# Two mixture layers: the turned and split x made once and read twice, and the top-8 taken in the logits' stage

## The chip, the cores and the metric

The program runs on one core of a Trainium2 chip. The metric is the device time of one launch in microseconds (us). The engines named below are PE (TensorE: matmuls and transposes), ACT (ScalarE), DVE (VectorE), POOL (GpSimd) and SP (SyncE, which only issues DMAs here).

## What is computed

Two transformer layers over 4096 tokens of width D = 256. Each is an attention followed by a mixture of experts, with a layer norm ahead of and behind each part. The change touches the mixtures alone. m0 is the mixture of the first layer and m1 that of the second:

```python
# m0 (xt: normalised tokens, H = 256, I = 512, E = 8, TOP_K = 2)
shared = jax.nn.silu(xt @ sg_w.T) * (xt @ su_w.T) @ sd_w.T
logits = xt @ router_w.T + routing_bias
topk_p, topk_idx = jax.lax.top_k(jax.nn.sigmoid(logits), TOP_K)
topk_p = topk_p / jnp.sum(topk_p, axis=-1, keepdims=True)
# routed = the experts' gated MLPs weighted by topk_p; output = shared + routed

# m1 (D = 256, routed H = 192, shared 2 * 192 = 384 wide, E = 8, K = 2, no bias)
scores = jax.nn.softmax((xf @ gate_w.T).astype(jnp.float32), axis=-1)
top_vals, top_idx = jax.lax.top_k(scores, K)
z = einsum(w_dense, experts) + _gated_mlp(xf, Ws1, Ws2)
```

## The kernel before

Tokens lie in T = 32 tiles of P = 128 rows. `core.x` and `core.y` are two arrays of 32 tiles that stay in on-chip memory (SBUF). x holds the running residual and y the output of a part until it is normed and added. Precision is kept by splitting: each float32 factor becomes a 16-bit high part and a 16-bit low part (what is left of it), and a product is three matmuls (high·high, low·high, high·low) or four.

One mixture runs five stages one after the other, each a block in which every engine has its own straight list of work, with semaphores between the lists. In the order of the profile's names, with m0's prefix:

- `m0ws` splits the shared expert's and the router's weights.
- `m0rl` (`router_logits`, from L2214) makes the router's logits. The 32 tiles go in 16 groups of two. Per group, DVE normalises two tiles (L2278), PE transposes them in four 128x128 blocks (L2235), ACT copies the transposes out of PSUM as the high part (L2269), DVE takes the low part (L2286), and PE multiplies both with the router in 32 matmuls of 8 columns each, 16 a tile (L2247). The high and low parts `m0rl_xt_high` and `m0rl_xt_low` have two buffers, which the next groups overwrite. DVE's list goes norm of group g+1, low of group g. PE's list goes turn of g+1, multiply of g. All 32 tiles' logits gather in one PSUM bank and DVE takes them out at the end in one instruction (L2303).
- `m0r` (`route`, from L2059) turns the logits into a place for every row in the experts' order. It is nearly all one chain on DVE. The bias row comes by a DMA that this stage issues and is added (L2139, m0 only). Then 32 MAX8 (L2142) give the eight largest logits of every token of a tile, and 32 max_index (L2145) their places. From L2147 on follow the counts and slots. Before its first instruction DVE waits for six constants that POOL makes (L2102 to L2110).
- `m0fs` (`shared_expert`, from L1597) runs the shared expert over 32 tiles in *slots* of one tile each. Beside it POOL sends each normalised row to its two places in `x_rows` in device memory (L1672), and SP, ACT and DVE load and split the routed experts' weights (`m0w_all`, L1707 and L1765), one piece per slot.
- `m0fx` (`routed_experts`) reads the sorted rows back and runs the routed experts.

In slot i of the shared expert, PE does the gate half of the up product of tile i, then its linear half (L1807, 24 matmuls of 128 columns each in m0, 18 in m1), then the transposes of tile i+2 (L1797, two per tile, called *turn*), then the down product of tile i-1 (L1807, 12 matmuls of 256 columns in m0, 9 in m1). ACT does silu of the gate (L1697), a weight piece's high part (L1707), a copy of tile i+2's normalised rows for the second send (L1692), the high part of its transposes (L1684) and the high part of the hidden values (L1703). DVE does the output of tile i-2 into y (L1760), the norm of tile i+3 (L1734), the weight piece's low part (L1765), silu times linear (L1748), the low part of the transposes of tile i+2 (L1741) and the low part of the hidden values (L1755). So every tile is normalised, transposed and split twice per mixture: once in `m0rl` and once in `m0fs`.

Turns of four slots are the unit of code: the first turn is written out, the other seven run in a hardware loop (`Fori`), and two closing slots follow. The logits' stage has such a loop too (six passes over two groups). Every engine's list is fixed by the code, so an engine that waits holds back all that stands behind it in its list.

## Time and profile before

| | us |
|---|---|
| median of 3 runs (2046.53 to 2051.81) | 2046.61 |
| the profiled execution, its own time | 2046.28 |
| its span in the trace | 2044.1 |

The sum of the prediction is made against the profiled execution, 2046.28 us. That is 0.33 us under the median, and 2.2 us of it lie around the span. The stages that the change touches, by the trace, from the first engine's entry to the next stage:

| stage | from to (us) | length |
|---|---|---|
| m0 logits | 256.0 to 284.8 | 28.8 |
| m0 route | 284.8 to 309.0 | 24.2 |
| m0 shared expert | 309.0 to 450.0 | 141.0 |
| m1 logits | 1635.5 to 1664.5 | 29.0 |
| m1 route | 1664.5 to 1686.5 | 22.0 |
| m1 shared expert | 1686.5 to 1814.0 | 127.5 |

Together they are 372.5 us of the span, and the rest of the program is the same code before and after. In the profile's rows an instruction stands with its start, its length, its engine and line, what it writes and reads, and, in brackets, how long the engine had been idle before it and what ended the wait. "issue" there means that nothing the profile shows was waited for, and "remote" that the last event came from elsewhere than a named instruction.

### The profile page before, as it was taken

The page shows a single profiled execution, that of the slowest core. Times are in us where ns is not written, and L with a number is a line of the kernel's source. Part 1 is how long each engine was busy: PE and PEld are TensorE (multiplying, and loading weights), DVE is VectorE, ACT ScalarE, POOL GpSimd, SP SyncE. Part 2 cuts the span into 40 slices and gives each one's busy share as a digit, 9 for nine tenths or more (in the row PEclk, how much of TensorE's full clock was granted, in tenths as well). Part 3 has the DMA queues.
Part 4 walks back from the last instruction along what each step waited for, and adds up shares of the span by engine and source line. Part 5 has one row for each costly group of instructions (what it writes and reads, how often), then busy time and mean ns, then how long its engine had stood idle before and what let it go on. Part 6 is the DMA issues. An engine that isn't in the chain of part 4 may idle for free. (4 is left out here: it accounts for less than half of the span.)

```text
span 2044.1 us, 43859 instructions
## 1 busy us (share of the span) xinstructions
PE 1667.6 (82%) x15250; PEld 953.9 (47%) x15250; DVE 1477.2 (72%) x2895; ACT 1098.1 (54%) x2248; POOL 418.3 (20%) x533
## 2 busy tenths in 40 slices
PE   2897259999999993767999999999997358889950
PEld 1775148976666662321222222222225247767740
DVE  4776677764444446869999999999936776656657
ACT  1443415643333332534999999999993415444422
POOL 2000206631222222220000000000000206534432
PEclk9998759999999996776999999999998759999985
DMA  5600004541111113332121111120005003323445
GB/s 200 276 0 6 31 1 153 157 125 48 60 58 61 58 53 127 119 94 54 37 60 48 47 47 45 48 60 24 17 17 175 24 1 110 113 87 120 126 148 174
DMA packets 113033, 164.09 MB, mean 80 GB/s; under 512 B 20246, under 2 KB 89756, under 8 KB 110556
## 3 DMA queue, kind: packets, MB, share of 16 engines
q1 hardware_dynamic: 97340, 117.85, 19.1%
q0 software_dynamic: 15520, 43.93, 5.9%
q8 instruction: 109, 1.79, 0.4%
q14 instruction: 64, 0.52, 0.1%
HBM read 89.07 MB, written 72.37 MB: 79 GB/s over the span
## 5 line engine op out<-in xcount | busy, mean ns | idle before, releaser
L1499 DVE TENSOR_REDUCE sa_row_max<-psum 128x1 f32<-128x1024 f32 x512 | 582.5, 1217 | 12.3 <-PE psum L1381 12.2
L1482 ACT ACTIVATE sa_probs<-psum 128x512 f32<-128x512 f32 x1024 | 549.6, 597 | 37.8 <-PE psum L1432 28.3
L1381 PE MATMUL psum<-v_k_max,v_q_stack 48*128 48x512 f16 x1024 | 301.4, 398 | 24.4 <-DVE sa_row_max L1499 16.2
L1412 PE MATMUL psum<-sa_probs,sa_v_now 128*32 128x256 f32 (+1 forms) x3840 | 321.0, 406 | 0.1
L1432 PE MATMUL psum<-v_q_stack,sa_k_main 49*128 49x512 f16 x1024 | 309.8, 384 | 2.0 <-ACT sa_probs L1482 1.2
L1993 PE MATMUL psum<-m0w_all,m0fx_xt_high 128*128 x568 | 193.4, 382 | 0.6 <-DVE m0fx_xt_low L1925 0.6
L1432 PEld LDWEIGHTS psum<-v_q_stack,sa_k_main 49*128 49x128 f16 x1024 | 64.6, 94 | 222.3 <-ACT sa_probs L1482 208.5
L1412 PEld LDWEIGHTS psum<-sa_probs,sa_v_now 128*32 128x32 f32 x3840 | 75.7, 108 | 189.9 <-issue 100.1
L1939 DVE TENSOR_TENSOR m0fx_ht_low<-psum,m0fx_ht_high 128x512 f16<-128x512 f32 x71 | 49.1, 692 | 134.4 <-ACT m0fx_ht_high L1907 134.4
L1901 ACT ACTIVATE m0fx_gate<-psum 128x512 f32<-128x512 f32 x71 | 42.4, 598 | 152.7 <-PE psum L1993 148.4
L1884 POOL DMA_INDIRECT y_rows<-m0fx_y_sb,m0fx_x_in x71 | 68.3, 962 | 274.1 <-DVE m0fx_y_sb L1946 274.1
L1306 POOL TENSOR_SCALAR sa_max_half<-sa_o_sb 128x128 f16<-128x128 f32 x32 | 9.3, 291 | 553.0 <-ACT sa_o_sb L1473 553.0
L1993 PE MATMUL psum<-m0w_all,m0fx_xt_low 128*128 x284 | 108.5, 382 | 0.0
L1993 PE MATMUL psum<-m0w_all,m0fx_ht_high 128*128 x568 | 104.6, 273 | 0.2 <-DVE m0fx_ht_low L1939 0.2
L1807 PE MATMUL psum<-m0fs_xt_high,m0s_all 128*128 128x128 f16 x1024 | 91.0, 220 | 1.3 <-issue 0.7
L1884 POOL DMA_INDIRECT y_rows<-m1fx_y_sb,m1fx_x_in x71 | 68.3, 962 | 102.3 <-DVE m1fx_y_sb L1946 101.1
L1807 PE MATMUL psum<-m0fs_xt_low,m0s_all 128*128 128x128 f16 x512 | 88.7, 220 | 0.4 <-issue 0.4
L1672 POOL DMA_INDIRECT x_rows<-m0fs_x_in,m_slots x64 | 75.8, 1184 | 47.6 <-ACT m0fs_x_in L1692 32.5
L1993 PE MATMUL psum<-m1w_all,m1fx_xt_high 128*128 x284 | 81.9, 330 | 0.6 <-DVE m1fx_xt_low L1925 0.6
L1807 PEld LDWEIGHTS psum<-m0fs_xt_high,m0s_all 128*128 128x128 f16 x1024 | 80.8, 99 | 2.1 <-DVE m0fs_xt_low L1741 0.9
L1993 PEld LDWEIGHTS psum<-m0w_all,m0fx_xt_high 128*128 128x128 f16 x568 | 56.0, 99 | 53.3 <-issue 2.7
L1381 PEld LDWEIGHTS psum<-v_k_max,v_q_stack 48*128 48x128 f16 x1024 | 55.0, 94 | 55.2 <-DVE sa_row_max L1499 46.7
(371 smaller groups left out, 3737.6 us busy)
## 6 DMA issues: line engine op xcount, KB each, us to landing
x_rows<-la_blank SPq DMA_DIRECT2D x18, 1032.0 KB, 8.2
v_q_stack<-q_scratch SPq DMA_DIRECT2D x192, 64.0 KB, 2.4
m0fx_x_in<-x_rows SPq DMA_DIRECT2D x71, 129.0 KB, 2.0
m1fx_x_in<-x_rows SPq DMA_DIRECT2D x71, 129.0 KB
m0fs_stage<-in_up SPq DMA_DIRECT2D x16, 512.0 KB
m0g_got<-y_rows SPq DMA_DIRECT2D x32, 256.0 KB, 3.8
o_scratch<-sa_o_sb POOLq DMA_DIRECT2D x32, 256.0 KB, 2.5
wo_o_in<-o_scratch SPq DMA_DIRECT2D x32, 256.0 KB, 3.6
```

Of the source, the lines that this page charges most:

```text
L1306: nc.gpsimd.tensor_scalar(max_half[n % 2][:, :], o_sb[n % 2][:, 0:P], 1.0 / MAX_SCALE, 1.0, ALU.mult, ALU.mult).then_inc(s["max_rounded"], 1)
L1381: nc.tensor.matmul(mx_ps[m % 2][:, half * 512:(half + 1) * 512], q_stack[h][side:side + ROWS, head, qt * P:(qt + 1) * P], k_max[side:side ...
L1412: last = nc.tensor.matmul(o_ps[32 * g:32 * g + 32, cols], v_now[:, kt, kv, :], probs[(GROUPS * step + g) % 16][:, cols], start=(kt == 0), ...
L1432: nc.tensor.matmul(st_ps[bank_of(at)][:, :], k_main[rows, kv, kt * P:(kt + 1) * P], q_stack[h][rows, kv * GROUPS + g, :], start=True, stop ...
L1482: nc.scalar.activation(probs[at % 16][:, :], st_ps[bank_of(at)][:, :], ACT.Exp, scale=0.25 / (QK_SCALE * QK_SCALE)).then_inc(s["expd"], 1)
L1499: nc.vector.tensor_reduce(row_max[n % 2][:, at % QT, column:column + 1], mx_ps[m % 2][:, :], AX.X, ALU.max).then_inc(s["maxed"], 1)
L1672: pool.indirect_dma_start(flat_rows, bass.IndirectOffsetOnAxis(ap=r.slots[:, i, c:c + 1], axis=0), x_in[i % UNROLL][:, c, :], None)\
L1807: last = nc.tensor.matmul(out, left(a, k), right(b, k), start=(m == 1), stop=(m == 3 * blocks))
L1884: pool.indirect_dma_start(y_rows, bass.IndirectOffsetOnAxis(ap=x_in[i % ROWS_HELD][:, D:D + 1].bitcast(I32), axis=0), y_sb[i % 2][:, :], N ...
L1901: nc.scalar.activation(gate[j][:, :], gate_ps[j][:, 0:F], ACT.Silu, scale=1.0 / W_SCALE)\
L1939: nc.vector.tensor_tensor(ht[j][1][0:ROWS, :, :], blocks(ht_ps[0:ROWS, 0:KF * P]), ht[j][0][0:ROWS, :, :], ALU.subtract).then_inc(s["ht_lo ...
L1993: last = nc.tensor.matmul(out, left(a, k), right(b, k), start=(m == 1), stop=(m == 3 * stop_at))
```

## The change

- `core.xt` is a second view of y: the 1024 bytes that a row of a tile has in y hold the high and the low part of its transposed tile, as 16-bit numbers.
- In the logits' stage, ACT's high part and DVE's low part go there, for all 32 tiles, and stay. PE reads them there in the logits' matmuls and again in the shared expert. When the shared expert's output of tile i-2 is done, it overwrites the tile's place in y.
- In the shared expert the transposes, their high part, their low part, two PSUM banks and three semaphores go. PE waits for neither the norm nor the split of a tile. Norm, copy and send of the rows to `x_rows` stay.
- The loops of the logits' stage and of the shared expert are written out on every engine. In the shared expert that is eight turns instead of one and a loop, and the two closing slots.
- The logits of each eight tiles (a *round* of four groups) go to one of two PSUM banks. DVE takes them out with the scale and the bias (`keep`, one instruction on 128x64), and does their 8 MAX8 (`maxima`) and 8 max_index (`find`). These three follow the low parts of groups 4q+5, 4q+6 and 4q+7 for rounds q = 0 to 2, and come at the end of the list for round 3.
- The bias row's DMA is issued at the start of the logits' stage. `route` loses it, the addition, and all MAX8 and max_index. It starts with what was L2147.

```diff
         self.y = ctx.enter_context(nc.sbuf_tensor("y", [P, T, D], F32))
+        self.xt = self.y[:, :, :].bitcast(F16).rearrange("p t (a k q) -> p t a k q", a=2, k=KD)
...
-    PEELED = 1
...
-        xt = [[ph.sb(f"xt_{x}{j}", [P, KD, P], F16) for x in ("high", "low")] for j in range(2)]
...
-        xt_ps = [ph.ps() for j in range(2)]
...
-            for k in range(PEELED):
-                turn(k)
-            with eng.Fori(PEELED, TURNS - PEELED) as k:
-                turn(k)
-            for k in range(TURNS - PEELED, TURNS):
+            for k in range(TURNS):
...
-                def high(i, j):
-                    act.wait_ge(s["x_turned"], i + 1)
-                    ge(act, s["lined"], i - 1)
-                    nc.scalar.activation(xt[j][0][:, :, :], xt_ps[j][:, 0:D].rearrange("p (k t) -> p k t", k=KD),
-                                         ACT.Copy).then_inc(s["xt_high"], 1)
...
                         again(i + 2, u + 2, k)
-                        high(i + 2, j)
...
-                    ge(dve, s["x_turned"], i - (UNROLL - 1))
                     ge(dve, s["x_again"], i - (UNROLL - 1))
...
-                def low(i, j):
-                    dve.wait_ge(s["xt_high"], i + 1)
-                    ge(dve, s["lined"], i - 1)
-                    nc.vector.tensor_tensor(xt[j][1][:, :, :], xt_ps[j][:, 0:D].rearrange("p (k t) -> p k t", k=KD),
-                                            xt[j][0][:, :, :], ALU.subtract).then_inc(s["xt_low"], 1)
...
-                    if real(i + 2):
-                        low(i + 2, j)
...
-                def turn(i, j, w):
-                    pe.wait_ge(s["x_ready"], i + 1)
-                    ge(pe, s["xt_low"], i - 1)
-                    for k in range(KD):
-                        last = nc.tensor.transpose(xt_ps[j][:, k * P:(k + 1) * P], x_in[w % UNROLL][:, 0, k * P:(k + 1) * P],
-                                                   core.ident[:, :])
-                    last.then_inc(s["x_turned"], 1)
...
-                def up(out, j, column):
+                def up(out, i, column):
...
-                                     lambda b, k: xt[j][b][:, k, :], KD)
+                                     lambda b, k: core.xt[:, i, b, k, :], KD)
...
                     if real(i):
-                        pe.wait_ge(s["xt_low"], i + 1)
                         ge(pe, s["silu_done"], i - 1)
-                        up(gate_ps[j], j, F).then_inc(s["gated"], 1)
+                        up(gate_ps[j], i, F).then_inc(s["gated"], 1)
                         ge(pe, s["hidden_done"], i - 1)
-                        up(lin_ps[j], j, 0).then_inc(s["lined"], 1)
-                    if real(i + 2):
-                        turn(i + 2, j, u + 2)
+                        up(lin_ps[j], i, 0).then_inc(s["lined"], 1)
                     if real(i - 1):
...
-            @block.sync
-            def _(sp):
-                if bias_row is not None:
-                    sp.dma_start(bias[:, :], bias_row.to_broadcast([P, E])).then_inc(bias_in, 16)
...
-                if bias_row is not None:
-                    dve.wait_ge(bias_in, 16)
-                    then(nc.vector.tensor_tensor(r.logits[:, :, :], r.logits[:, :, :],
-                                                 bias[:, :].unsqueeze(1).to_broadcast([P, T, E]), ALU.add))
-                for t in range(T):
-                    last = nc.vector.max(top[:, t, :], r.logits[:, t, :])
-                then(last)
-                for t in range(T):
-                    last = nc.vector.max_index(index[:, t, :], top[:, t, :], r.logits[:, t, :])
-                then(last)
...
+    ROUND = 4
+    xt = core.xt
...
+        def part(g, a):
+            return xt[:, g * G:(g + 1) * G, a, :, :].rearrange("p u k t -> p u (k t)")
...
+                def multiply(g):
                     pe.wait_ge(s["low"], g + 1)
+                    if g % ROUND == 0:
+                        ge(pe, s["kept"], g // ROUND - 1)
...
+                for g in range(NG):
+                    if g + 1 < NG:
+                        turn(g + 1)
+                    multiply(g)
...
+                    nc.scalar.activation(part(g, 0), turned(g % 2), ACT.Copy).then_inc(s["high"], 1)
...
+                    nc.vector.tensor_tensor(part(g, 1), turned(g % 2), part(g, 0), ALU.subtract).then_inc(s["low"], 1)
...
+                def keep(q):
+
+                    dve.wait_ge(s["logged"], (q + 1) * ROUND)
+                    at = slice(q * ROUND * G, (q + 1) * ROUND * G)
+                    given = logit_ps[q % 2][:, 0:ROUND * G * E].rearrange("p (t e) -> p t e", e=E)
+                    if bias_row is not None:
+                        ge(dve, s["bias_in"], 16)
+                        nc.vector.scalar_tensor_tensor(out=logits[:, at, :], in0=given, scalar=1.0 / W_SCALE,
+                                                       in1=bias[:, :].unsqueeze(1).to_broadcast([P, ROUND * G, E]),
+                                                       op0=ALU.mult, op1=ALU.add).then_inc(s["kept"], 1)
+                    else:
+                        nc.vector.tensor_scalar(logits[:, at, :], given, 1.0 / W_SCALE, None, ALU.mult)\
+                            .then_inc(s["kept"], 1)
+
+                def maxima(q):
+                    dve.wait_ge(s["kept"], q + 1)
+                    for t in tiles_of(q):
+                        last = nc.vector.max(top[:, t, :], logits[:, t, :])
+                    last.then_inc(s["maxed"], 1)
+
+                def find(q):
+                    dve.wait_ge(s["maxed"], q + 1)
+                    for t in tiles_of(q):
+                        last = nc.vector.max_index(index[:, t, :], top[:, t, :], logits[:, t, :])
+                    last.then_inc(s["found"], 1)
+                norm(0)
+                for g in range(NG):
+                    if g + 1 < NG:
+                        norm(g + 1)
+                    low(g)
+                    q, at = divmod(g - ROUND - 1, ROUND)
+                    if q >= 0:
+                        (keep, maxima, find)[at](q) if at < 3 else None
+                keep(NG // ROUND - 1)
+                maxima(NG // ROUND - 1)
+                find(NG // ROUND - 1)
+                dve.wait_ge(s["found"], NG // ROUND)
```

Three places of the order. On DVE in m0's logits stage, the loop's pass over two groups (its ISA rows are register instructions) before:

```order
L2278 TENSOR_SCALAR m0rl_xhat1<-x,mean_var,rstd 128x256
L2278 ISA x2
L2278 TENSOR_SCALAR m0rl_xhat1<-x,mean_var,rstd 128x256
L30 REGISTER_ALU
L2286 TENSOR_TENSOR m0rl_xt_low0<-psum,m0rl_xt_high0 128x512
L2278 ISA x2
L2278 TENSOR_SCALAR m0rl_xhat0<-x,mean_var,rstd 128x256
L2278 ISA x2
L2278 TENSOR_SCALAR m0rl_xhat0<-x,mean_var,rstd 128x256
L2286 TENSOR_TENSOR m0rl_xt_low1<-psum,m0rl_xt_high1 128x512
L2293 REGISTER_ALU
L2293 COMPARE_AND_BRANCH
```

and after, from the norm of group 6 to that of group 9, with the first round's three steps among them:

```order
L2227 TENSOR_SCALAR m0rl_xhat0<-x,mean_var,rstd 128x256 x2
L2233 TENSOR_TENSOR y<-psum,y 128x2x256
L2245 SCALAR_TENSOR_TENSOR m0rl_logits<-psum,m0rl_bias 128x64
L2227 TENSOR_SCALAR m0rl_xhat1<-x,mean_var,rstd 128x256 x2
L2233 TENSOR_TENSOR y<-psum,y 128x2x256
L2255 MAX m0l_top<-m0rl_logits 128x8 x8
L2227 TENSOR_SCALAR m0rl_xhat0<-x,mean_var,rstd 128x256 x2
L2233 TENSOR_TENSOR y<-psum,y 128x2x256
L2261 MAX_INDEX m0l_index<-m0l_top,m0rl_logits 128x8 x8
L2227 TENSOR_SCALAR m0rl_xhat1<-x,mean_var,rstd 128x256 x2
```

The low part now goes to y, and behind the low parts of groups 5, 6 and 7 stand the keep, the eight MAX8 and the eight max_index of tiles 0 to 7, ahead of the next norm.

On DVE in m0's shared expert, the first slot and the start of the second, before:

```order
L1734 TENSOR_SCALAR m0fs_x_in3<-x,mean_var,rstd 128x256
L1765 SCALAR_TENSOR_TENSOR m0w_all<-m0fs_stage,m0w_all 128x1024
L1748 SCALAR_TENSOR_TENSOR m0fs_hidden0<-psum,m0fs_gate0 128x512
L1741 TENSOR_TENSOR m0fs_xt_low0<-psum,m0fs_xt_high0 128x256
L1755 TENSOR_TENSOR m0fs_ht_low0<-m0fs_hidden0,m0fs_ht_high0 128x512
L1734 TENSOR_SCALAR m0fs_x_in0<-x,mean_var,rstd 128x256
L1765 SCALAR_TENSOR_TENSOR m0w_all<-m0fs_stage,m0w_all 128x1024
L1748 SCALAR_TENSOR_TENSOR m0fs_hidden1<-psum,m0fs_gate1 128x512
```

and after:

```order
L1718 TENSOR_SCALAR m0fs_x_in3<-x,mean_var,rstd 128x256
L1743 SCALAR_TENSOR_TENSOR m0w_all<-m0fs_stage,m0w_all 128x1024
L1726 SCALAR_TENSOR_TENSOR m0fs_hidden0<-psum,m0fs_gate0 128x512
L1733 TENSOR_TENSOR m0fs_ht_low0<-m0fs_hidden0,m0fs_ht_high0 128x512
L1718 TENSOR_SCALAR m0fs_x_in0<-x,mean_var,rstd 128x256
L1743 SCALAR_TENSOR_TENSOR m0w_all<-m0fs_stage,m0w_all 128x1024
L1726 SCALAR_TENSOR_TENSOR m0fs_hidden1<-psum,m0fs_gate1 128x512
```

The low part of the transposes is gone from between the product of silu and linear half and the hidden low part.

On PE in m0's shared expert, the end of the second slot, before (last up matmuls, turn of tile 3, down of tile 0):

```order
L1807 MATMUL psum<-m0fs_xt_high,m0s_all 128x128 x2
L1807 MATMUL psum<-m0fs_xt_low,m0s_all 128x128
L1797 MATMUL psum<-ident,m0fs_x_in 128x128 x2
L1807 MATMUL psum<-m0s_all,m0fs_ht_high 128x256
L1807 MATMUL psum<-m0s_all,m0fs_ht_low 128x256
L1807 MATMUL psum<-m0s_all,m0fs_ht_high 128x256 x2
```

and after, the third slot from its 48 up matmuls on, which now read y:

```order
L1772 MATMUL psum<-y,m0s_all 128x128 x48
L1772 MATMUL psum<-m0s_all,m0fs_ht_high 128x256
L1772 MATMUL psum<-m0s_all,m0fs_ht_low 128x256
L1772 MATMUL psum<-m0s_all,m0fs_ht_high 128x256 x2
L1772 MATMUL psum<-m0s_all,m0fs_ht_low 128x256
L1772 MATMUL psum<-m0s_all,m0fs_ht_high 128x256 x2
L1772 MATMUL psum<-m0s_all,m0fs_ht_low 128x256
```

The two transposes between the up and the down product are gone. The down product follows the linear half.

## Rows read from the trace of the kernel before

**Rows 1.** Windows: stretch and length, then busy time per engine (instructions), clock, DMA.

```profile
core 0: us, PE busy (x) PEld busy (x) DVE busy (x) ACT busy (x) POOL busy (x), PEclk, DMA share, GB/s
...
256.00:284.80 28.80, 24.83 (x320) 20.48 (x320) 21.47 (x49) 9.55 (x16) 0.00 (x0) 0.50 0.00 1
...
309.00:450.00 141.00, 137.65 (x1984) 131.12 (x1984) 104.76 (x190) 82.55 (x161) 84.07 (x95) 0.99 0.49 150
...
1686.50:1814.00 127.50, 113.09 (x1504) 101.38 (x1504) 81.48 (x190) 63.77 (x161) 72.04 (x95) 0.98 0.33 104
```

**Rows 2.** Groups by line, first logits stage: group, count, busy, mean ns, idle before.

```profile
L2286 DVE TENSOR_TENSOR m0rl_xt_low<-psum,m0rl_xt_high 128x512 f16<-128x512 f32 x16 | 11.1, 691 | 6.6 <-ACT m0rl_xt_high L2269 6.6
...
L2303 DVE TENSOR_SCALAR m_logits<-psum 128x256 f32<-128x256 f32 x1 | 0.4, 426 | 0.7 <-PE psum L2247 0.7
```

**Rows 3.** Timeline of DVE, first logits stage: start, us, instruction, [idle before <-releaser].

```profile
275.16 0.69 DVE L2286 TENSOR_TENSOR m0rl_xt_low<-psum,m0rl_xt_high 128x512 f16<-128x512 f32 x1 [0.68 <-ACT m0rl_xt_high L2269]
...
276.47 0.69 DVE L2286 TENSOR_TENSOR m0rl_xt_low<-psum,m0rl_xt_high 128x512 f16<-128x512 f32 x1
...
278.50 0.69 DVE L2286 TENSOR_TENSOR m0rl_xt_low<-psum,m0rl_xt_high 128x512 f16<-128x512 f32 x1 [0.67 <-ACT m0rl_xt_high L2269]
```

**Rows 4.** Timeline, start of both routing stages, to where their max_index runs end.

```profile
286.55 0.29 POOL L2110 TENSOR_SCALAR_AFFINE_SELECT m0r_before<-m0r_before 128x128 f32<-128x128 f32 x1
...
287.98 0.42 DVE L2139 TENSOR_TENSOR m_logits<-m_logits,m0r_bias 128x256 f32<-128x256 f32 x1 [3.14 <-DMA m0r_bias<-in_bias_r]
...
295.22 0.20 DVE L2147 CAST m0r_index_f<-m0r_index 128x64 f32<-128x64 uint32 x1
...
1666.16 0.58 DVE L2142 MAX8 m1r_top<-m_logits 128x8 f32<-128x8 f32 x7 [1.78 <-POOL m1r_before L2110]
...
1672.95 0.20 DVE L2147 CAST m1r_index_f<-m1r_index 128x64 f32<-128x64 uint32 x1
```

**Rows 5.** Timeline of PE, first work of the first shared expert.

```profile
308.84 1.12 PE L1797 MATMUL psum<-ident,m0fs_x_in 128*128 128x128 f32 x4 [9.98 <-DVE m0fs_x_in L1734]
...
310.46 0.39 PE L1807 MATMUL psum<-m0fs_xt_high,m0s_all 128*128 128x128 f16 x2 [0.51 <-DVE m0fs_xt_low L1741]
```

**Rows 6.** Timeline of PE, first shared expert: one turn and two slot ends.

```profile
353.40 0.39 PE L1797 MATMUL psum<-ident,m0fs_x_in 128*128 128x128 f32 x2
...
353.63 0.28 PE L1807 MATMUL psum<-m0s_all,m0fs_ht_high 128*128 128x256 f16 x1
...
354.84 0.27 PE L1807 MATMUL psum<-m0s_all,m0fs_ht_high 128*128 128x256 f16 x1
...
359.06 0.27 PE L1807 MATMUL psum<-m0s_all,m0fs_ht_high 128*128 128x256 f16 x1
```

**Rows 7.** Timeline of ACT, silu of two slots of the first shared expert.

```profile
352.71 0.58 ACT L1697 ACTIVATE m0fs_gate<-psum 128x512 f32<-128x512 f32 x1
...
356.80 0.58 ACT L1697 ACTIVATE m0fs_gate<-psum 128x512 f32<-128x512 f32 x1
```

**Rows 8.** Timeline of PE, second shared expert: last down matmuls of slots.

```profile
1705.41 0.27 PE L1807 MATMUL psum<-m1s_all,m1fs_ht_high 128*128 128x256 f16 x1
...
1708.63 0.27 PE L1807 MATMUL psum<-m1s_all,m1fs_ht_high 128*128 128x256 f16 x1
...
1808.66 0.27 PE L1807 MATMUL psum<-m1s_all,m1fs_ht_high 128*128 128x256 f16 x1
```

**Rows 9.** Waits in the second shared expert: us in total, times, longest.

```profile
ACT m1fs_xt_high L1684 <- remote: 17.3, 8, 3.3
...
PE psum L1807 <- issue: 9.0, 26, 0.5
...
PE psum L1807 <- DVE m1fs_ht_low L1755: 4.0, 9, 1.0
```

**Rows 10.** Waits in the first shared expert, same columns.

```profile
PEld psum L1807 <- issue: 1.7, 4, 0.5
```

**Rows 11.** Groups by line, second shared expert, the row scatter.

```profile
L1672 POOL DMA_INDIRECT x_rows<-m1fs_x_in,m_slots x64 | 65.5, 1024 | 47.1 <-ACT m1fs_x_in L1692 27.8 <-issue 8.0 <-DVE m1fs_x_in L1734 6.6
```

105 lines of the change are left out of this document (35 added, 70 removed).

## The prediction

> **What bounds the kernel now.** I read the table of windows first, stage by stage, since the share of busy time over the whole span mixes stages with different limits. In the first shared expert PE is busy 137.65 of 141.00 us at a clock of 0.99, and DVE, the next, 104.76 [rows 1]. So PE's list is the stage, and what leaves that list shortens it. In the second shared expert PE is busy 113.09 of 127.50 us: PE is still the longest list, but something stops it. In the logits stage PE (24.83) and DVE (21.47 of 28.80 us) are both high at half the clock, 0.50 [rows 1]. There I went to the groups by line and the timeline of DVE: before every second low part DVE waits 0.67 to 0.68 us for ACT's high part, nine times with 6.6 us in all [rows 2, 3]. So neither engine is full. A loop through PE, ACT and DVE sets the pace, 3.34 us for two groups (275.16 to 278.50). In the route stage all is one chain on DVE, so its rows can be subtracted one by one [rows 4].
>
> **Route: what goes.** In m0 the stage comes to the cast of the indices (L2147) at 295.22. What that cast needs besides the indices is POOL's last constant, done at 286.55 + 0.29 = 286.84 [rows 4]. The bias wait (3.14 us of idle), the addition, the 32 MAX8 and the 32 max_index lie between. So up to 295.22 - 286.84 = 8.4 us go. In m1 there is no bias and the constants have already been waited for: 1672.95 - 1666.16 = 6.8 us go [rows 4]. The bias DMA moves to the start of the logits stage, more than 10 us ahead of its first use, with nothing else in SP's list there: nothing. Together -15.2 us.
>
> **Logits: what comes.** MAX8 and max_index cost 6.79 / 32 = 0.212 us a tile [rows 4], 1.70 us for a round of eight. The keep of 128x64 has no row. It lies between nothing and the 0.43 of the keep of 128x256 [rows 2]; I take 0.20, the cast of the same shape [rows 4]. A round is 1.9 us. Rounds 0 to 2 (5.7 us) stand between the low parts, where DVE idles 2 x 0.68 us in four groups [rows 3], 4.1 us beside three rounds. If all idle time takes them, 5.7 - 4.1 = 1.6 us remain; if none, 5.7. A low part that is late delays PE's next turn and so the whole loop, and the two longer steps come singly in front of a norm, so one idle time does not cover a step wholly. I take 3.2, nearer to the low end, since the idle time is in the same list right behind. Round 3 stands at the end with nothing beside it: 1.9 less the old keep of 0.43, that is 1.5. Each logits stage gets 4.7 us longer (3.1 to 7.2), both 9.4 (6.3 to 14.4). Logits and route together: -15.2 + 9.4 = **-5.8 us** (-8.9 to -0.8).
>
> **First shared expert.** The turn's two transposes take PE from 353.40 to 353.63, that is 0.23 us [rows 6]. They stand in 30 of the 32 slots: 30 x 0.23 = 6.9 us, and the slot of 359.06 - 354.84 = 4.22 becomes 3.99. At the start the first transposes run at 308.84 and the first up matmul waits for the split until 310.46 [rows 5]. Up to 1.6 us of this go, less because the first matmuls then run longer at the low clock of the stages ahead; I take 1.2 (0.8 to 1.6). PE's queue stood still four times without a releaser, 1.7 us in all [rows 10]; as written-out code may keep or lose that, I take 0.9 (0 to 1.7). What is late next is the ring through ACT and DVE: silu, weight piece high, weight piece low, product, hidden high, silu. Between two silus it takes 356.80 - 352.71 = 4.09 us where the piece is 1024 wide [rows 7], 0.10 over the new 3.99. This ring loses from its ACT list the high part of the transposes and from its DVE list the low part, but both stand where these engines wait for each other, so I grant nothing. Half of the pieces are 1024 wide, so up to 16 x 0.10 = 1.6 us come back; since the two PSUM buffers let the narrow pieces make up for the wide ones, I take 0.5. Sum: -6.9 - 1.2 - 0.9 + 0.5 = **-8.5 us** (-10.2 to -6.1).
>
> **Second shared expert.** The same turns, -6.9, and the same start, -1.2. Then the waits. From 1705.41 to 1808.66 PE does 27 slots in 103.25 us [rows 8]. An undisturbed slot is 1708.63 - 1705.41 = 3.22, so 86.9 would do and 16.3 us are lost. 4.0 of them are PE waiting for the hidden low part, 9 times, and ACT waits in the same stage 17.3 us in 8 long waits that end with no named instruction, about one for each of the loop's seven passes and its entry [rows 9]. I read these as one thing: ACT comes late behind the loop's edge, then DVE, then PE. Written out there is no edge, so 4.0 go (bound: 0). The other 12.3 us are stand-stills of PE's own queue in the midst of a product ("issue", 9.0 us in 26 waits on the matmuls' row alone [rows 9]). No semaphore of the change touches these, so in the likeliest case I let them stay. Sum: -6.9 - 1.2 - 4.0 = **-12.1 us** (-8.1 if the waits stay).
>
> **The sum.** 2046.28 - 5.8 - 8.5 - 12.1 = **2019.9 us**, with its own bounds 2046.28 - 8.9 - 10.2 - 12.1 = 2015 and 2046.28 - 0.8 - 6.1 - 8.1 = 2031. The median of before is 0.33 us above the profiled execution, far inside these bounds.
>
> **Rival 1: the stand-stills of m1 go with the loop.** If PE's queue runs dry because of the loop's edges, 12.3 us more go: 2007.6. For it speaks that they hit the matmuls of m1's stage, most of which run in the loop. Against it: m0's stage has the same loop around the same kind of matmuls and shows four short ones [rows 9, 10]. The Trainium skill, Runtime: NRT & Kernel Launch, section Instruction fetch mechanics, states that an engine fetches its code ahead only in sequence, that a taken branch out of the fetched window makes it wait, and that kernels therefore prefer full unrolling; by that rule the time would be this rival's. The trace agrees with it in m1 only and not in m0.
>
> **Rival 2: writing out brings stand-stills, and the kernel is slower.** m1's slots lose 12.3 / 27 = 0.46 us each without a releaser. If what starves PE there is new code at a high rate of short instructions, then all 64 slots read new code after the change, while before only the first turns and the loop's first pass did. If m0's slots only reach m1's rate, 32 x 0.46 = 14.6 us come back: 2034.5, still faster. It decides from (26.4 + 6.1) / 64 = 0.51 us more in every slot of both mixtures on; with one us lost in every slot, m0 gains 32 and m1 17 us and the time is 2046.3 - 26.4 + 49 = 2069. Against it: m0's first turn is written out already, and its whole stage has four such waits [rows 10].
>
> **Rival 3: the row scatter becomes the bound in m1.** PE's slot there would be 3.22 - 0.23 = 2.99. POOL is busy 72.04 / 32 = 2.25 us a tile [rows 1], of which the two sends are 65.5 / 32 = 2.05 [rows 11], and every tile has three hand-overs between POOL, ACT and DVE. If these make a tile 3.22 long, DVE's norm (it waits until its buffer has been sent) holds up the hidden values behind it in DVE's list and the turns' 6.9 us are not gained: 2026.8. For it: a tile's steps come one after the other. Against it: 47.1 us of POOL's idle time, much of it waiting for ACT [rows 11], which loses work.
>
> **How the numbers follow.** Likeliest case 0.48 (2015 to 2031), rival 1 0.22 (2003 to 2010), rival 3 0.10 (2022 to 2031), m0 at m1's rate of stand-stills 0.08 (2030 to 2037). About 0.3% is what a measurement of this kernel can tell from no change. Within it (2040 to 2052) lies rival 2 with 0.35 to 0.6 us a slot, 0.07. Beyond it, slower, 0.05. So faster 0.88, same 0.07, slower 0.05. The range 2004 to 2034 leaves out the last two, a part of the m0 case and the low end of rival 1, together under 2 in 10.
>
> **What would show it.** Right: last down matmuls of neighbouring slots 3.99 apart in m0 and 2.99 in m1 where nothing stands; DVE's cast of the indices within 2 us of the route block's start; logits stages of 32 to 36 us; in m1 still some 20 "issue" waits of PE. Wrong: m0's slots at 4.1 or more (the ring binds), POOL with no idle time in m1 (rival 3), PE's "issue" waits gone (rival 1) or many of them in m0 (rival 2), or a logits stage over 36 us, where DVE would be the bound.

## The result

| | us |
|---|---|
| before, median of 5 runs (2046.53 to 2051.81) | 2049.20 |
| after, median of 4 runs (2028.17 to 2034.33) | 2031.59 |
| ratio after / before, 95% interval | 0.9913 (0.9893 to 0.9933) |
| forecast, ratio to the profiled run | 2019.9, 0.987 |

A fifth run of after took 4100.99 us at a granted clock of 1.0, which nothing here explains, and is left out.

The change is faster by 0.87% (0.67 to 1.07), 17.6 us by the medians. It was to be 26.4 us. The sign was right and the time lies within the range that was given, but a third of the expected gain is missing. The profiled execution of after took 2032.23 us (span 2030.2), so in the traces the gain is 13.9 us of span.

The profiled run of before, 2046.28 us, lies under all five timed ones. The first part of the program, which the change doesn't touch, took 243.1 us in it and 244.2 to 247.9 in the traces of all other kernels here.

This is the table of windows of after, the six touched stages in the order of [rows 1], with the columns of that group:

```profile
core 0: us, PE busy (x) PEld busy (x) DVE busy (x) ACT busy (x) POOL busy (x), PEclk, DMA share, GB/s
257.60:290.90 33.30, 24.61 (x320) 20.71 (x320) 28.16 (x148) 9.55 (x16) 0.00 (x0) 0.50 0.01 2
290.90:306.00 15.10, 2.12 (x6) 1.28 (x7) 11.17 (x40) 0.42 (x1) 1.22 (x7) 0.50 0.00 1
306.00:443.00 137.00, 132.12 (x1920) 124.96 (x1919) 93.94 (x160) 72.46 (x129) 79.65 (x96) 0.99 0.53 156
1629.30:1662.60 33.30, 24.62 (x320) 20.72 (x320) 28.16 (x148) 9.55 (x16) 0.00 (x0) 0.50 0.00 1
1662.60:1677.20 14.60, 2.05 (x5) 1.21 (x6) 10.68 (x38) 0.42 (x1) 1.15 (x7) 0.50 0.00 0
1677.20:1797.00 119.80, 107.47 (x1440) 96.89 (x1440) 69.25 (x160) 54.12 (x129) 73.96 (x96) 0.95 0.36 112
```

The same stages from the first instruction of each to the first of the next, before and after, from the timelines, with a second trace of after (experiment *again*):

| stage | before | after | again | change | forecast |
|---|---|---|---|---|---|
| m0 logits | 29.5 | 33.4 | 33.4 | +3.9 | +4.7 |
| m0 route | 22.9 | 14.6 | 14.6 | -8.4 | -8.4 |
| m0 shared expert | 142.9 | 137.8 | 141.6 | -5.1, -1.3 | -8.5 |
| m1 logits | 29.6 | 33.4 | 33.4 | +3.7 | +4.7 |
| m1 route | 21.0 | 14.2 | 14.2 | -6.8 | -6.8 |
| m1 shared expert | 129.1 | 120.4 | 124.0 | -8.8, -5.1 | -12.1 |
| sum | 375.1 | 353.7 | 361.1 | -21.3, -13.9 | -26.4 |
| all the rest of the span | 1669.0 | 1676.5 | 1671.1 | +7.4, +2.0 | 0 |

Route came as forecast and logits 0.8 to 1.0 us a stage better, and both repeat to 0.1 us. What is missing is missing in the shared experts, and these differ by 3.6 to 3.9 us each from one trace of the same kernel to the next. The rest of the span, whose code is the same, is longer by 2 to 7 us. Its parts moved the same way in unrelated kernels: m1's routed experts took 162.0 to 165.7 us over the fourteen traces, 162.8 before and 165.7 after.

In the logits stage of m0, on the timeline of DVE (start, length, instruction, idle time before it):

```profile
268.20 0.69 DVE L2233 TENSOR_TENSOR y<-psum,y 128x512 f16<-128x512 f32 x1
268.81 0.21 DVE L2245 SCALAR_TENSOR_TENSOR m0rl_logits<-psum,m0rl_bias 128x64 f32<-128x64 f32 x1
...
270.62 0.64 DVE L2255 MAX8 m0l_top<-m0rl_logits 128x8 f32<-128x8 f32 x8
...
276.06 0.69 DVE L2233 TENSOR_TENSOR y<-psum,y 128x512 f16<-128x512 f32 x1 [0.59 <-ACT y L2219]
...
286.92 0.69 DVE L2233 TENSOR_TENSOR y<-psum,y 128x512 f16<-128x512 f32 x1 [0.69 <-ACT y L2219]
```

The keep takes 0.21 us and eight MAX8 0.64. DVE waits before seven of the low parts instead of nine, 4.6 us in all where it was 6.6 [rows 2]:

```profile
L2233 DVE TENSOR_TENSOR y<-psum,y 128x512 f16<-128x512 f32 x16 | 11.0, 691 | 4.6 <-ACT y L2219 4.5
```

From the stage's start to its last low part it is 29.05 us against 27.15 before, so rounds 0 to 2 added 1.9 us where 3.2 were taken and 1.6 was the lower bound. From that low part to the route stage it is 4.38 against 2.36: the tail added 2.0 instead of 1.5, since round 2's max_index also stand behind the last low part (286.92). Ahead of the first keep two groups take 3.17 to 3.18 us (low parts at 260.49, 263.67 and 266.84) where they took 3.34 to 3.35 before (258.45, 261.80, 265.14): this stage's own pace is a little faster after the change, which the sum had at nothing; what makes it so was not taken apart. In the route stages, the first rows on DVE are these:

```profile
292.78 0.20 DVE L2088 CAST m0r_index_f<-m0l_index 128x64 f32<-128x64 uint32 x1 [2.05 <-POOL m0r_before L2061]
...
1664.17 0.20 DVE L2088 CAST m1r_index_f<-m1l_index 128x64 f32<-128x64 uint32 x1 [1.78 <-POOL m1r_before L2061]
```

They answer to [rows 4]: DVE now waits for POOL's last constant and nothing else.

PE's waits in the two shared experts, m0 first, then m1 (us in total, times, longest):

```profile
PE psum L1772 <- DVE m0fs_ht_low L1733: 3.3, 9, 1.3
...
PE psum L1772 <- issue: 1.1, 4, 0.4
```

```profile
PE psum L1772 <- issue: 5.9, 18, 0.5
...
PE psum L1772 <- DVE m1fs_ht_low L1733: 5.0, 8, 1.2
```

They answer to [rows 10] and [rows 9]. The waits for the hidden low part, of which m1's 4.0 us were to go, are 5.0 us now in m1, and 3.3 in m0 where they were 1.7.

### The profile page after: what moved, and what is told of

The parts are those of the page before. It is cut to its first block and busy times, and to the rows that moved or that the text cites. A ratio compares the mean times of both kernels' runs of the same rounds, so it can differ in the third digit from the quotient of the medians.

```text
span 2030.2 us, 42355 instructions
## 1 busy us (share of the span) xinstructions
PE 1658.7 (82%) x15122; PEld 946.4 (47%) x15122; DVE 1451.0 (71%) x2836; ACT 1079.1 (53%) x2184; POOL 415.6 (20%) x533
## 3 DMA queue, kind: packets, MB, share of 16 engines
q1 hardware_dynamic: 97340, 117.85, 19.4%
## 5 line engine op out<-in xcount | busy, mean ns | idle before, releaser
L1772 PE MATMUL psum<-y,m0s_all 128*128 128x128 f16 x1536 | 93.3, 221 | 10.4 <-PEq L2050 9.5
L1772 PEld LDWEIGHTS psum<-y,m0s_all 128*128 128x128 f16 x1536 | 90.3, 99 | 12.3 <-issue 11.6
L1772 PE MATMUL psum<-y,m1s_all 128*128 128x128 f16 x1152 | 76.8, 225 | 14.5 <-PEq L2050 9.4
```

Source lines behind the costliest of these rows:

```text
L1772: last = nc.tensor.matmul(out, left(a, k), right(b, k), start=(m == 1), stop=(m == 3 * blocks))
```

## Where a slot loses time

The measure for all that follows is taken from the timeline of PE: the time from the last down matmul of slot 0 to that of slot 31, less what undisturbed slots would take. These are 3.99 us in m0 and 2.99 in m1 without the turns (4.22 and 3.22 with them), the last one 2.76 and 2.13 (2.35 and 1.98 where the hidden values go first). What is lost ahead of the end of slot 0 is not in this measure. The kernels marked "m1 only" differ from after in m1 alone, so their m0 is after's once more.

| kernel | m0: slot 0 to 31, lost | m1: slot 0 to 31, lost |
|---|---|---|
| before | 130.6, 1.8 | 117.5, 19.2 |
| after | 127.2, 4.8 | 111.2, 19.4 |
| again (after) | 130.8, 8.3 | 115.0, 23.2 |
| loops | 124.5, 2.1 | 119.1, 27.2 |
| ahead | 124.1, 2.0 | 110.4, 18.7 |
| spaced | 124.1, 1.7 | 111.1, 19.3 |
| ahead_spaced, best | 123.6 and 123.7, 1.6 and 1.7 | 112.1 and 111.4, 20.4 and 19.8 |
| before_spaced | 129.1, 0.3 | 111.9, 13.6 |
| old_shared | 131.9, 3.1 | 116.5, 18.2 |
| no_scatter (m1 only) | 131.7, 9.3 | 91.9, 0.1 |
| sp_sends (m1 only) | 129.3, 6.9 | 91.9, 0.1 |
| pool_plain (m1 only) | 126.9, 4.5 | 91.9, 0.1 |
| half_sends (m1 only) | 125.8, 3.3 | 91.9, 0.1 |

A stretch of after's m1 in which PE stands still, first POOL, then PE on the same microseconds:

```profile
1699.08 0.20 POOL L1660 COPY m1fs_x_in<-m_tail 128x4 f32<-128x4 f32 x1
1699.55 0.98 POOL L1666 DMA_INDIRECT x_rows<-m1fs_x_in,m_slots  x1 [0.28 <-issue]
1700.84 0.96 POOL L1666 DMA_INDIRECT x_rows<-m1fs_x_in,m_slots  x1 [0.30 <-issue]
1701.80 0.20 POOL L1660 COPY m1fs_x_in<-m_tail 128x4 f32<-128x4 f32 x1
1702.28 0.98 POOL L1666 DMA_INDIRECT x_rows<-m1fs_x_in,m_slots  x1 [0.28 <-issue]
```

```profile
1699.06 0.50 PE L1772 MATMUL psum<-y,m1s_all 128*128 128x128 f16 x6
1699.80 0.27 PE L1772 MATMUL psum<-y,m1s_all 128*128 128x128 f16 x2 [0.24 <-issue]
1700.51 0.27 PE L1772 MATMUL psum<-y,m1s_all 128*128 128x128 f16 x2 [0.44 <-issue]
1701.26 0.38 PE L1772 MATMUL psum<-y,m1s_all 128*128 128x128 f16 x4 [0.48 <-issue]
1702.00 0.22 PE L1772 MATMUL psum<-y,m1s_all 128*128 128x128 f16 x1 [0.36 <-issue]
1702.72 0.60 PE L1772 MATMUL psum<-y,m1s_all 128*128 128x128 f16 x4 [0.50 <-issue]
```

PE does one to six matmuls of a product, stands for 0.24 to 0.50 us with no semaphore to wait for, and does the next. Beside it POOL sends rows without a pause. In the windows around it (columns as in [rows 1]) it shows what that costs twice:

```profile
1690.00:1696.40 6.40, 6.32 (x94) 5.81 (x92) 3.45 (x9) 3.25 (x8) 5.22 (x8) 1.00 0.40 132
1696.40:1702.60 6.20, 3.57 (x32) 2.08 (x29) 1.76 (x4) 1.21 (x3) 4.75 (x8) 1.00 0.44 133
1702.60:1709.50 6.90, 6.08 (x44) 4.84 (x45) 3.78 (x9) 2.04 (x5) 3.17 (x4) 0.51 0.23 73
1709.50:1720.00 10.50, 10.07 (x151) 9.49 (x149) 5.52 (x12) 4.94 (x12) 6.56 (x9) 1.00 0.37 115
```

From 1696.4 to 1702.6 PE does 32 matmuls where the stretch before had 94 in about the same time, and then TensorE's granted clock is 0.51, the lower of its two levels, until 1709.5. Slot 5 takes 9.07 us.

## The experiments

The theories at the start were those of the prediction: stand-stills that go with the loop (rival 1), that come with new code (rival 2), the row sends as the bound (rival 3), and, for m0's longer slots, the wide weight pieces. Each kernel was timed beside before, and its ratio is to before's runs of that time.

**again.** The same kernel.

> The changed kernel once more, nothing altered, to see whether PE's stand-stills have a place. In its first trace the down products of slots 0 and 31 of the second shared expert end 111.2 us apart where 30 undisturbed slots of 2.99 and the last of 2.13 would take 91.8: 19.4 us lost, 6.1 of them in slot 5 alone. In the first shared expert 127.2 against 122.5: 4.8 lost, 2.0 in slot 1. If the stand-stills belong to a place in the code: the same slots stand for about as long, slot 5 of m1 at 8 to 10 us, 17 to 21 us lost in m1. If they come from what else happens to go on at that moment: other slots stand, and the loss differs by several us. Time 2028 to 2034 us either way.

Measured: 2036.95 us (2031.55 to 2040.42) where before took 2050.36, ratio 0.9919 (0.9892 to 0.9947). Now slot 1 of m0 takes 9.55 and slot 1 of m1 8.44 us, and m1's slot 5 takes 4.47. So the stand-stills have no fixed place in the code. They come in the first slots, more often than not, and then in changing places of m1.

**loops.** One part of the change undone:

```diff
-            for k in range(TURNS):
+            turn(0)
+            with eng.Fori(1, TURNS - 1) as k:
                 turn(k)
+            turn(TURNS - 1)
```

> The changed kernel, but with the shared expert's hardware loop kept: first and last turn written out, six passes between, PE reading y by the loop's counter. If m1's stand-stills come from the loop's edges (rival 1 of the prediction), writing out should have removed them, which it did not; then this kernel loses about as much as the changed one or more, 19 to 25 us in m1, plus about 4 us of waits of PE for the hidden low part behind the edges: 3 to 8 us slower than the changed kernel. If they come from fresh code (rival 2), code that repeats has few: under 10 us lost in m1 and under 3 in m0, 8 to 12 us faster than the changed kernel. If they depend on neither: within 3 us of it.

Measured: 2035.67 us, ratio 0.9918 (0.9890 to 0.9947), beside again's 0.9919. PE's waits in m1:

```profile
PE psum L1774 <- issue: 12.7, 39, 0.4
...
PE psum L1774 <- DVE m1fs_ht_low L1735: 3.9, 8, 1.0
```

The loop has 27.2 us of loss in m1 (again 23.2, after 19.4). In m0 it has 2.1 (8.3 and 4.8), but slot 0 ends 12.2 us into the stage (after 9.2, again 9.6), since PE waits 2.92 us there for the hidden low part. Writing the shared expert out is worth nothing that these runs can tell, and code that repeats stands still as often as new code. Rivals 1 and 2 both fall.

**ahead.** ACT's and DVE's slots in another order:

```diff
 # ACT
                         silu(i, j)
-                        cut_high(k, u)
                     if real(i + 2):
                         again(i + 2, u + 2, k)
                     if real(i):
                         hidden_high(i, j)
+                        cut_high(k, u)
 # DVE
+                    if real(i):
+                        multiply(i, j)
                     if real(i - 2):
                         finish(i - 2, j)
                     if real(i + 3):
                         norm(i + 3, u + 3, k)
                     if real(i):
-                        cut_low(k, u)
-                    if real(i):
-                        multiply(i, j)
-                    if real(i):
                         hidden_low(i, j)
+                        cut_low(k, u)
```

> The changed kernel, but in each slot of the shared expert the hidden values go ahead of the weight piece: ACT does silu, row copy, hidden high, weight piece high; DVE does silu times linear, output of tile i-2, norm of tile i+3, hidden low, weight piece low. Same instructions, other order. In the changed kernel's trace every fourth slot of m0 takes 4.32 to 4.37 instead of 3.99 us, with PE waiting for the hidden low part (3.3 us in m0, 5.0 in m1). If that comes from the two wide weight pieces that stand in the way of the hidden values (the ring that the prediction priced at 0.5 us): m0's slots all become 3.99, 2.5 to 3.3 us less in m0, 3 to 5 less in m1, 5 to 8 us faster than the changed kernel. If PE's waits only follow from its own stand-stills, or the weight pieces now come late: no gain, or the next stage starts later, within 2 us of it. The stand-stills without a releaser (13 to 15 us in m1) stay in both.

Measured: 2023.67 us (2020.74 to 2026.65), 13 us less than again beside it, where 5 to 8 were expected. The ratio to before, 0.9847, has a wide interval (0.9774 to 0.9920). All slots of m0 but slot 4 (6.01 us) are 3.99. In m1 18.7 us are still lost.

**no_scatter.**

```diff
                     for c in range(2):
...
+                        if filled is None:
+                            nc.gpsimd.memset(unsent[:, 2 * i + c:2 * i + c + 1], 0.0).then_inc(sent[i % UNROLL], 16)
+                            continue
                         pool.indirect_dma_start(flat_rows,
```

> The changed kernel without the sends of rows to x_rows in m1 alone; the POOL instructions that sent are replaced by a memset of one column each. It leaves out that the second mixture's routed experts see the rows, so their part of the output is not computed. If the sends (64 indirect DMAs beside PE's stream, and the descriptors that POOL writes for them) make PE's queue stand still in m1: its loss falls from 19.4 to under 5 us and the time by 12 to 17 us. If rival 3 (the scatter as the bound) holds, PE's waits for the hidden low part go with it, 5 us. If neither: 15 us or more are still lost without a releaser, and the time changes by less than 4 us.

Measured: 2012.51 us. The window of m1's shared expert:

```profile
1680.80:1781.50 100.70, 97.86 (x1440) 93.92 (x1440) 69.74 (x160) 55.05 (x129) 10.85 (x96) 0.98 0.17 49
```

That is 100.7 us instead of 119.8, every slot 2.99, 0.1 us lost, and the waits for the hidden low part are down to two, 1.8 us in all. So all of m1's stand-stills come with the sends, and the waits are for the most part their shadow.

**spaced.** One wait more on POOL:

```diff
                     ge(pool, sent[i % UNROLL], i // UNROLL * 32)
+                    ge(pool, s["gated"], i - 1)
                     nc.gpsimd.tensor_copy(x_in[i % UNROLL][:, :, D:ROW], r.tail[:, i, :, :]).then_inc(s["tail_set"], 1)
```

> The changed kernel with one wait more on POOL: before tile i's row copy and two sends it waits until PE has done the gate product of tile i-2, so that the sends come two per slot with a pause behind them and never four or more in a row. Every row is still sent. Without any sends in m1 its loss there was 0.1 us instead of 19 to 23, so the sends make PE stand; the gaps in the traces lie on the third and later of sends that follow each other in 1.3 to 1.5 us. If the run of sends is what counts: m1 loses under 5 us, the clusters in the first slots of m0 (2 to 6 us) go too, and the time falls by 12 to 20 us against the changed kernel, to 2012 to 2020. If the mere number of sends counts: still over 12 us lost in m1, and no gain.

Measured: 2025.73 us, ratio 0.9887 (0.9857 to 0.9918). The windows of the two shared experts:

```profile
304.90:439.60 134.70, 130.83 (x1920) 125.20 (x1920) 93.17 (x160) 72.87 (x129) 77.45 (x96) 0.98 0.54 158
```

```profile
1672.20:1792.70 120.50, 106.54 (x1440) 96.55 (x1440) 69.73 (x160) 54.16 (x129) 70.96 (x96) 0.96 0.36 111
```

Half right. m0 is 134.7 us long, and apart from slot 1 (5.65) all its slots are 3.99. m1 still loses 19.3 us, where under 5 were expected. But there the wait did not make the pause that it was for. POOL and PE in m1, as POOL comes to send two pairs one behind the other:

```profile
1694.61 0.96 POOL L1667 DMA_INDIRECT x_rows<-m1fs_x_in,m_slots  x1 [0.30 <-issue]
...
1696.22 0.98 POOL L1667 DMA_INDIRECT x_rows<-m1fs_x_in,m_slots  x1 [0.46 <-issue]
1697.51 0.96 POOL L1667 DMA_INDIRECT x_rows<-m1fs_x_in,m_slots  x1 [0.30 <-issue]
```

```profile
1698.29 0.49 PE L1773 MATMUL psum<-y,m1s_all 128*128 128x128 f16 x6 [0.32 <-issue]
1699.03 0.89 PE L1773 MATMUL psum<-y,m1s_all 128*128 128x128 f16 x13 [0.24 <-issue]
```

Call it a run where sends start less than 1.8 us after one another. m1 of *spaced* has nine runs of four or more sends, and the like kernels *ahead_spaced* and *best* below have ten and nine. All of PE's "issue" waits there (24, 31 and 28) lie between the third send of a run and 1.5 us behind its last, a stretch of about a third of the stage, and every run has some. Pairs that stand alone have none. In m1 of after (18 waits), again (27) and before (26) too, all lie in runs of three or more. So where PE stands speaks for the run, and m1's loss does not speak against it. A pair needs 2.7 us (1.29 and 1.44 from send to send), so a slot of 2.99 leaves hardly any pause. No kernel here makes pauses in m1 with both indirect sends, so rate and run are not told apart by a test of their own.

*spaced* also takes away what *ahead* was to explain. After has 4.32 to 4.37 us in every fourth slot of m0 (again up to 4.41), and the wide weight pieces are the same in spaced. The rows of ACT, first of after, then of spaced, at such a slot:

```profile
343.95 0.60 ACT L1685 ACTIVATE m0fs_gate<-psum 128x512 f32<-128x512 f32 x1 [1.48 <-PE psum L1772]
344.45 1.05 ACT L1695 ACTIVATE m0w_all<-m0fs_stage 128x1024 f16<-128x1024 f32 x1
...
347.93 0.58 ACT L1685 ACTIVATE m0fs_gate<-psum 128x512 f32<-128x512 f32 x1
```

```profile
341.44 0.60 ACT L1686 ACTIVATE m0fs_gate<-psum 128x512 f32<-128x512 f32 x1 [0.88 <-PE psum L1773]
341.93 1.05 ACT L1696 ACTIVATE m0w_all<-m0fs_stage 128x1024 f16<-128x1024 f32 x1
...
345.43 0.60 ACT L1686 ACTIVATE m0fs_gate<-psum 128x512 f32<-128x512 f32 x1
```

From silu's start to the end of the hidden low part it is 4.84 us in after and 4.82 in spaced, and from silu to silu 3.98 and 3.99. The ring keeps up, but with nothing to spare at a slot of 3.99. What differs is silu's start: 0.86 us behind the gate product's last matmul in after, 0.26 in spaced, with nothing in the rows that ACT could have waited for. It is the same in all of these slots of after (six) and again (seven): silu comes 0.81 to 0.90 us behind that matmul, and the second of two sends 1.46 us apart starts 0.58 us ahead of it. In spaced the second send starts 1.6 us ahead of that matmul in the same slots, and silu comes 0.26 us behind it. So the delay goes with where the sends lie, and the ring without slack passes it on to PE. How a send reaches ACT was not taken apart.

**before_spaced.** The same wait in the kernel before.

> The kernel before the change with the same one wait on POOL. It shows what the change is worth where nothing stands still. If runs of sends made the stand-stills of before too: m1 loses under 5 of its 16 to 18 us over slots of 3.22, m0's 1.8 at slot 3 go, and the time is 2026 to 2034. The change between the two spaced kernels is then what the prediction's sum gives without stand-stills and with the late hidden parts: 9 us less for logits and route, 6 to 8 for m0's shared expert, 7 to 10 for m1's, some 22 to 26 in all. If the wait holds the turns up (PE reads the norm's buffer here, which is only free after a send): slower than 2040.

Measured: 2040.53 us, ratio 0.9960 (0.9946 to 0.9974). m0 loses 0.3 us, m1 13.6. Between the two spaced kernels the change is worth 14.8 us, not 22 to 26: m0's shared expert 6.8 and logits with route 7.5 by the traces, but m1's shared expert only 2.6. From slot 0 to 31 m1 takes 111.9 us with the turns and 111.1 without.

**ahead_spaced, best.** Both edits together, timed twice.

> The two edits together: hidden values ahead of the weight pieces, and sends at the pace of the slots. Hidden first alone gave about 10 us against the changed kernel. If the causes are separate (weight pieces in the way of the hidden values in m0; runs of sends that stop PE in m1 and in the first slots), every slot of both mixtures is undisturbed: m0's slots all 3.99 and m1's all 2.99, under 2 us lost in each, 2004 to 2012 us. If m1's waits for the hidden low part were only the shadow of the sends, the sum is less than both: 2012 to 2018.

> The kernel of ahead_spaced again (hidden values ahead of the weight pieces, sends at the pace of the slots), timed in more rounds beside the kernel before. The changed kernel stood at 0.9913 and 0.9919 of before. If the two edits add something that can be measured: 0.985 to 0.989 of before. m0's slots are 3.99 but for one of the first three; m1 again loses about 20 us, since two sends a slot are still more than PE bears.

Measured: 2023.40 us, ratio 0.9873 (0.9850 to 0.9895), and 2021.76 us, ratio 0.9879 (0.9859 to 0.9899). Both lie above what was expected of the two edits. They add nothing to each other that can be measured (ahead 2023.67, spaced 2025.73): each alone has made all of m0's slots but one whole, and neither helps m1. This is a version ahead of both kernels, 24 and 28 us under before by the medians.

**sp_sends, pool_plain, half_sends.** What about the sends stops PE. In m1, SP sends the same bytes to a fixed place; or POOL does so with plain DMAs; or POOL makes one of the two indirect sends. The first two leave out that the rows go to their experts' places, the third the second copy of each row. The edits, with SP's and the counters' waits left out here:

```diff
 # sp_sends, behind each weight piece on SP
...
+                                sp.dma_start(x_rows[2 * i + c, :, :], x_in[i % UNROLL][:, c, :])\
+                                    .then_inc(sent[i % UNROLL], 16)
 # pool_plain
+                            pool.dma_start(x_rows[2 * i + c, :, :], x_in[i % UNROLL][:, c, :])\
+                                .then_inc(sent[i % UNROLL], 16)
 # half_sends
                             pool.wait_ge(s["x_again"], i + 1)
+                            if filled is None:
+                                continue
...
```

> The changed kernel, in m1 with the same rows and bytes sent by SP's plain DMAs, tile after tile in a fixed place of x_rows, in place of POOL's indirect DMAs. It leaves out that the rows go to their experts' places, so the routed part of the second mixture is not what it should be. If it is the bytes moved beside PE's stream (129 KB twice a slot) that stop PE: the loss in m1 stays over 12 us. If it is what POOL does to send by a list of places (its own instruction of about 1 us, with descriptors made there): the loss falls to under 3 us as without sends, and m1's stage is 100 to 103 us long.

> The changed kernel, in m1 with the same rows and bytes sent by POOL's plain DMAs to a fixed place, as SP did it in the run before with 0.1 us lost. It leaves out that the rows go to their experts' places, so the routed part of the second mixture is not what it should be. If POOL making the descriptors is what stops PE, whatever the list: over 10 us lost in m1 again. If only the indirect form does (its list of places, row by row): under 3 us lost.

> The changed kernel with one of the two sends of each tile in m1. It leaves out that m1's rows reach their second expert, so the routed part of the second mixture is not what it should be. Without sends or with plain ones from SP, m1 lost 0.1 us; with two a slot (2.99 us) 19 to 23, with or without a pause between slots; m0, with two in 3.99 us, loses under 2 when they are spaced. If there is a rate below which sends cost PE nothing (between 0.50 a us, m0's, and 0.67, m1's): one per 2.99 us, 0.33 a us, loses under 1 us. If each send costs PE something: half of the loss, 9 to 11 us, stays.

Measured: 2011.49, 2011.33 and 2010.70 us. The windows of m1's shared expert in sp_sends, pool_plain and half_sends, in this order:

```profile
1679.90:1780.80 100.90, 98.87 (x1440) 95.12 (x1440) 69.96 (x160) 55.07 (x129) 6.72 (x32) 0.97 0.48 133
```

```profile
1679.40:1780.30 100.90, 97.82 (x1440) 93.90 (x1440) 69.74 (x160) 55.07 (x129) 40.95 (x96) 0.98 0.47 133
```

```profile
1677.60:1778.90 101.30, 97.94 (x1440) 94.02 (x1440) 69.06 (x160) 55.04 (x129) 38.86 (x64) 0.98 0.30 91
```

All three lose 0.1 us. In the first two DMA is busier than in after (0.48 and 0.47 against 0.36), with 133 GB/s against 112, so it isn't the bytes. POOL's groups, first after's indirect sends, then pool_plain's:

```profile
L1666 POOL DMA_INDIRECT x_rows<-m1fs_x_in,m_slots x64 | 65.4, 1022 | 38.0 <-ACT m1fs_x_in L1680 19.8 <-issue 9.4 <-POOL m1fs_x_in L1660 5.6
```

```profile
L1667 POOL DMA_DIRECT2D x_rows<-m1fs_x_in x64 | 34.7, 542 | 50.9 <-ACT m1fs_x_in L1684 40.8 <-POOL m1fs_x_in L1660 9.2 <-DVE m1fs_x_in L1722 0.8
```

The queue that took them, first in after's m1, then in pool_plain's (packets, MB, share of the DMA engines' time):

```profile
q0 software_dynamic: 3072, 8.46, 19.6%
```

```profile
q0 software_dynamic: 3072, 8.46, 21.9%
```

The same packets and bytes on the same queue, two a slot, stop nothing when they are sent plainly. So something in the indirect form counts, and not that POOL issues it. What it is stays open: the list, the scattered places, or the length of a send. The plain send holds POOL for 0.54 us and the indirect one for 1.02, so behind a plain pair the next send starts 1.8 to 2.1 us later. Only at the stage's start do nine plain sends follow each other at 0.5 to 1.4 us, and PE has no "issue" wait there. The Trainium skill, DMA: Bandwidth & Descriptors, section SWDGE vs HWDGE vs iDMA, says that for any DMA issued from GpSimd a program there writes the descriptors, and for one from SP hardware does; if such a program's work were enough to stop PE, pool_plain would have stood like after, and it lost 0.1 us. Half as many indirect sends, one in 2.99 us and so never in a run behind the first four, cost PE 0.1 us.

**old_shared.** The logits and route of the change with the shared expert of before.

> The kernel before the change with the change's logits and route stages alone; the shared expert turns, splits and loops as before. The stages read from the changed kernel's trace give for this part: logits 3.9 and 3.7 us longer, route 8.4 and 6.8 shorter, 7.5 us together (the prediction had 5.8). Expected: 5 to 9 us faster than before, 2040 to 2044 where before is 2047 to 2050. If more of the whole gain sits here (the shared experts' stages of the changed kernel gain 5.1 and 8.8 us in one trace, but 1.3 and 5.1 in the second), the shared part is near nothing: 10 us or more faster.

Measured: 2041.05 us, ratio 0.9949 (0.9929 to 0.9969), 8 us by the medians. About half of the change's 13 to 18 us is this part, as the traces say (7.5).

## Why the prediction was right and where it was not

- **Route (right).** 15.1 us measured for 15.2. A chain on one engine could be subtracted row by row.
- **Logits (right within its bounds, the split not as taken).** 7.7 us for 9.4. The idle times gave 2.0 us (6.6 to 4.6) where 2.5 were granted. What the sum did not have is the stage's quicker pace, 3.17 to 3.18 us for two groups where it had kept 3.34. The tail cost 0.5 us more, as round 2's max_index stand in it.
- **Start of the shared experts (under-sized).** From a stage's first instruction to the last down matmul of slot 0, m0 went from 10.98 to 9.22 and m1 from 10.39 to 7.89 us: 1.8 and 2.5 gained for 1.2 each.
- **m0's slots (the term was right, the rest of the sum wrong).** The slot did become 3.99. But 4.8 us (8.3 in the second trace) are lost where 1.8 were before, so that of 6.9 us of turns 3.4 and then nothing showed. Two steps failed. The 0.9 us granted for stand-stills did not come: slots 1 and 2 of after lose 2.7 us, and slot 1 of again 5.6 with the clock's fall behind it, where before lost 1.8. (The 1.7 us of [rows 10] are those of the weight loads; the matmuls themselves stood for 1.1.) The sends of the first tiles come without a pause there. And 2.1 us (2.7 in again) went in every fourth slot, which the prediction had priced at 0.5 and put down to the ring of the wide pieces alone. *spaced* shows the ring whole with these pieces; it is a late silu that it cannot take up.
- **m1's slots (wrong by mechanism).** "No semaphore of the change touches these, so in the likeliest case I let them stay" held in size, 19.2 us lost before and 19.4 after, and that is why the turns' part showed there in the first trace (117.5 to 111.2). But the 4.0 us of waits that were to go with the loop stayed (5.0): they are 1.8 us without the sends, so most of them were shadows of the stand-stills, and *loops* (3.9) shows that the loop's edge had no part in them. The match of ACT's eight waits with the loop's seven passes and its entry doesn't hold, as the loop makes six. In the second trace 23.2 us were lost and 2.5 of the 6.3 us showed.
- **Rival 3** named the right engine, with the wrong mechanism. POOL doesn't hold DVE's norm back, which waits 0.2 us in after's m1 behind the stage's entry; its indirect sends stop PE's own queue. Its sign of being true, POOL without idle time, doesn't hold either: POOL is busy 73.96 of 119.8 us in after.
- **Rival 1**, with the rule on branches from the Trainium skill (Runtime: NRT & Kernel Launch, section Instruction fetch mechanics): no run here bears it out for this stage. Written out and looped, the medians of the kernel are 0.1% apart, and each ratio's interval reaches 0.3% to either side.
- **The base.** The sum stood on a profiled run 2.9 us under the median that five runs gave, and the untouched rest of the span came 2 to 7 us longer. The rest moves by as much between the two traces of after, so no run puts it down to the change. That the time still fell within the range owes something to the range's width: route and logits missed by 0.1 and 1.7 us, but each shared expert by 3 to 7.

One detail of the text ahead of the prediction was wrong: the shared expert's loop makes six passes, and its last turn is written out like the first. Only the reading of ACT's eight waits leaned on it.

## What to carry to other kernels

A stand-still of an engine "without a releaser" is a cost with a cause, and before a change makes that engine's list denser the cause should be found by taking neighbours away one at a time: here one run without the sends told what no wait in the trace named. Work that is taken off the bounding engine shows only as far as nothing else fills the gap, and what the gap had been shielding (here sends in a run) comes out. An edit that is meant to spread work should be checked in the trace for whether it did: the one wait on POOL made pauses in m0 and not in m1. When an engine has slack to place its work, put work for the critical chain first and bulk work (weight pieces, sends) behind it and at the pace of the slots: that gave about 8 us more than the change alone (0.9879 against 0.9919 of before).

## What the runs showed of the hardware that I had not expected

- POOL's indirect sends of 128 rows of 1032 bytes stop PE's queue in the midst of a product where three or more follow each other at 1.3 to 1.8 us. With two in a slot of 2.99 or 3.22 us such runs form, and 13.6 to 27 us of some 111 to 119 are lost. With two in 3.99 us and a pause behind each pair under 2 us are lost, in the run of the first sends, and with one in 2.99 us 0.1. Not every run stops PE: some in m0, and six of the eleven in after's m1, did not.
- Plain sends of the same bytes, from SP or from POOL, two in the same 2.99 us, stop nothing (0.1 us lost). What in the indirect form reaches PE's queue was not found; no run here took it apart further.
- A cluster of such stand-stills in the middle of a busy stage was followed by TensorE's lower clock: 0.51 for 6.9 us in after's m1, and 0.50 for 3.4 us in m0 of *again*. That this is why ten runs of one kernel spread over 9 us (2031.55 to 2040.42) is likely, and was not shown.
